# Matmuls of the identity issued at the matrix engine's long planned waits, in a four-layer transformer block over four sequences

## The chip, the cores and the metric

The kernel runs on one core of one Trainium2 chip. Its time is the device time of one execution in microseconds (us), the median over several executions. A core has a matrix engine, TensorE (PE in the profile; PEld is its loading of weights), a vector engine (DVE), a scalar engine (ACT), GpSimd (POOL), and SyncE (SP), which here only issues transfers. TensorE writes into PSUM, eight banks of 128 partitions by 2 KB (512 float32 columns each).

## What is computed

Four sequences of 1024 tokens with 256 features pass, each by itself, through causal attention, a gated feed-forward block, sliding-window attention (64 keys) and the same feed-forward block again, each behind a layer norm and with a residual sum:

```python
x = x + attn_a(layernorm(x))    # x @ W1 + b1; causal softmax, 16 heads of 16; @ Wp + bp
x = x + ffn(layernorm(x))       # silu(x @ Wg.T) * (x @ Wu.T) @ Wd.T; hidden 768, int weights / 127
x = x + attn_b(layernorm(x))    # window of 64 keys, the first 63 given as initial keys and values
x = x + ffn(layernorm(x))       # the same feed-forward weights
```

## The kernel before

The kernel counts eight "layers", numbered 0 to 7: for each sequence a causal attention with its feed-forward block (even numbers) and a sliding one with its own (odd numbers). Every float32 product that needs the precision is made from two parts, hi and lo, rounded apart.

**Events.** The work of a layer is cut into events, each with one or more steps on different engines. Those that matter here, by their letters in the code: `L` turns four normalised token tiles with eight transposes (line 1285); `L0` and `L1` come before attention for the two halves of the tokens, `L2` and `L3` before the feed-forward block. `Q` and `P` make queries, keys and values (L1337 to L1339, L1353 to L1356). `A` computes scores once for the row maxima, which DVE reduces (L1424 or L1390; L1019); `T` turns the maxima (L1581). `B` computes the scores again, transposed and with the maximum subtracted, for ACT's exponential (L1446; L1215), `V` weighs the values (L1474). Both run over eight groups of heads and token halves, so that `B(3,0)` is the first piece of group 3. `O` projects (L1493 to L1496), `G0` to `G11` are gate and up for twelve pieces of the hidden layer, six for each token half, eight matmuls of 512 columns each (L1514, L1515), then a Silu on ACT (L1253), a product on DVE (L1096), the hi part on ACT (L1268) and the lo part on POOL (L921). `W(h,p)` is the product with the down weights, 24 matmuls of 256 columns (L1529, L1534), which waits for the lo part of all six pieces of its half. The second half of the feed-forward block of one layer is interleaved with the start of the next layer (small letters `g`, `w`).

**Order.** A planner, `Plan.order` (line 418 and on), writes the order of every engine's steps and the PSUM banks of each event at build time. It holds a cost for each step (`steps`) and what each needs (`needs`), keeps `free[engine]` and `done[event, step]`, and picks greedily. A planned wait of TensorE is the difference between the start that it works out for the next PE step and `free["PE"]`. The plan exists in four versions: layer 0, odd layers, even layers, and layer 7. `released(bank)` is the planned time at which the holder of a bank has been read for the last time.

**Run.** TensorE's program walks that order in `run`. Each event waits for its inputs and, in `banks_free`, for the semaphores that tell that the former holders of its banks have been read (`BEFORE`, from `holders_before`). The program from `G0` of layer 0 on stands twice, behind a branch on a value read at run time: the second parts of the feed-forward weights are used only where they are not all zero. A check of 36 matmuls (L1559) of these second parts with themselves, and a maximum over the result, decides it.

Of the kernel before, what the change touches and what calls it, by code (L numbers as in the profile page):

```python
# [21 lines left out]
P = 128  # L22
# [3 lines left out]
W = 64  # L26
# [15 lines left out]
BANKS = 8  # L42
SWITCH = 0.1
REACH = 96
PIECES = 8
SET_BY_POOL = 19
LANDED = {('stats', 0): 0.0, ('stats', 1): 4.5, ('qkv',): 2.5, ('bq',): 4.0, ('att_b',): 7.5, ('bias',): 8.5, ('wp', 0): 8.5,
# [35 lines left out]
class Plan:  # L83
# [11 lines left out]
    def __init__(self, a):  # L95
        self.causal = a % 2 == 0
        self.opening, self.final = a == 0, a == LAYERS - 1
        if self.causal:
            self.keys = [range(4 * (hf + 1)) for hf in range(2)]
        else:  # L100
            self.keys = [range(4 * hf, 4 * hf + 5) for hf in range(2)]
        if self.causal:
            self.a_units = [[u for i in range(4 * hf, 4 * hf + 4) for u in self.units(i, self.a_width(i))]
                            for hf in range(2)]
        else:
            self.a_units = [[(i, 0, HG, REACH) for i in (4 * hf, 4 * hf + 2)] for hf in range(2)]
        self.b_units = [[u for j in self.keys[hf] for u in self.units(j, self.b_width(hf, j))]
                        for hf in range(2)]
        self.b_upto = [{j: 1 + max(n for n, u in enumerate(units) if u[0] == j) for j in keys}
                       for units, keys in zip(self.b_units, self.keys)]  # L110
        self.a_base = running([len(self.a_units[sg // 4]) for sg in range(SUPERS)])
        self.b_base = running([len(self.b_units[sg // 4]) for sg in range(SUPERS)])
        self.v_base = running([len(self.keys[sg // 4]) for sg in range(SUPERS)])
        self.key_tiles = [(sg, j) for sg in range(SUPERS) for j in self.keys[sg // 4]]
        self.chunks = 2 if self.causal else 3
        self.slots = 2 if self.causal else 4
        self.lns = [0, 1, 2, 3]
        self.tail = range(12 if self.final else 6)
        self.us, self.program, self.banks = self.order(LIKES[2 if self.opening else 0 if self.causal else 1])

    def units(self, tile, width):

# [296 lines left out]
    def order(self, like):  # L419
# [2 lines left out]
        free = {"PE": 0.0, "ACT": 2.0, "DVE": 2.0, "POOL": 3.0, "SP": 0.0}  # L422
        banks = {}
        holder = [None] * BANKS
        at_start = [0.0, 0.0, 0.0, 0.0, 1.0, 1.0, 2.0, 2.0]
        done, program = {}, {engine: [] for engine in free}
        if self.opening:
# [35 lines left out]
        while left:  # L463
            best = None
            for m, (events, n_steps) in enumerate(streams):
                for step in range(n_steps):
                    if at[m][step] == len(events) or step and at[m][step] >= at[m][step - 1]:
                        continue
                    e = events[at[m][step]]
                    kind = e[0]  # L470
                    steps = self.steps(e)
                    if step >= len(steps):
                        best = (-1.0, m, step, e, None, 0.0)
                        continue
                    needs = self.needs(e, step)
                    if any(x not in done for x in needs):
                        continue
                    start = max([free[steps[step][0]], done[e, step - 1] if step else 0.0] + [done[x] for x in needs])
                    if kind == "Z" and e[1] == 0 and not self.causal:
                        start = max(start, 3.0)  # L480
                    if kind == "g" and not step:
                        start = max(start, 1.0)
                    if not step and self.banks_of(e):
                        slot, _ = choice(e, start)
                        if slot is None:
                            continue
                        start = max(start, slot)
                    key = start - like[self.group_of(e)]
                    if steps[step][0] == "PE" and self.in_quarters(e) != quarters:
                        key += like["turn"]  # L490
                    if not step:
                        if kind in "AB":
                            key = max(key, free[steps[1][0]] - steps[0][1] - like[f"ahead{e[1] // 4}"])
                            if kind == "A" and reached["A"] > reached["B"] + like[f"lead{e[1] // 4}"]:
                                key += 1.5
                        if kind == "P" or kind == "Q" and e[2]:
                            key += -like["late"] if (("A", 0, 3 if self.causal else 1), 0) in done else 3.0
                    if best is None or key < best[0]:
                        best = (key, m, step, e, steps, start)
            key, m, step, e, steps, start = best  # L500
            at[m][step] += 1
            left -= 1
            if steps is None:
                continue
            engine, us, after = steps[step]
            if engine == "PE" and self.in_quarters(e) != quarters:
                quarters = not quarters
                us += SWITCH
            free[engine] = start + us
            done[e, step] = start + us + after  # L510
            program[engine].append((e, step))
            if not step:
                if self.banks_of(e):
                    banks[e] = choice(e, start)[1]
                    for bank in banks[e]:
                        holder[bank] = e
                if e[0] in reached:
                    hf = e[1] // 4
                    units = (self.a_units if e[0] == "A" else self.b_units)[hf]
                    reached[e[0]] = e[1] + (e[2] + 1) / len(units)  # L520
        self.done = done
        return max(free["PE"], free["ACT"] - 2.0, free["DVE"] - 2.0, free["POOL"] - 3.0,
                   done.get((("W", 0, 1), 1), 0.0) - 2.3), program, banks


_PLANS = {a: Plan(a) for a in (0, 1, 2, LAYERS - 1)}
# [11 lines left out]
def holders_before():  # L538


    held, out = {}, {}
    for a, plan in enumerate(PLANS):
        for e, step in plan.program["PE"]:
            if e in plan.banks and (a, e) not in out:
                out[a, e] = list(dict.fromkeys(held[bank] for bank in plan.banks[e] if bank in held))
                for bank in plan.banks[e]:
                    held[bank] = (a, e)
    return out


def next_tables():
# [4 lines left out]
    return {x: TABLES[y[1][0]] for x, y in zip(ops, ops[1:]) if TABLES[x[1][0]] != TABLES[y[1][0]]}  # L556


BEFORE = holders_before()
NEXT_TABLE = next_tables()  # L560


def layers_kernel(nc, x, att_a, att_b, b_qk, b_v, wp_a, wp_b, b_p, w_gu, w_dn, k_init, v_init, out):
# [5 lines left out]
    with ExitStack() as ctx:  # L569
# [71 lines left out]
        ident_b = sb("ident_b", [P, P], BF16)  # L641
# [637 lines left out]
        def _(pe):  # L1279
# [8 lines left out]

            def banks_free(a, e):


                for b, (kind, *n) in BEFORE.get((a, e), ()):
                    plan = PLANS[b]
                    if kind == "Q":
                        pe.wait_ge(part_rest, chunk(b, *n) + 2)
                    elif kind == "P":
                        pe.wait_ge(v_done, VALUE_DONE_BASE[b] + VALUE_DONE[b % 2][n[0]])
                    elif kind == "A":
                        pe.wait_ge(a_max, A_BASE[b] + plan.a_base[n[0]] + n[1] + 1)
                    elif kind == "T":  # L1300
                        pe.wait_ge(peak_done, SUPERS * b + n[0] + 1)
                    elif kind == "B":
                        pe.wait_ge(exp_done, B_BASE[b] + plan.b_base[n[0]] + n[1] + 1)
                    elif kind == "U":
                        if n[0] == "bias":
                            pe.wait_ge(s_bias, 3)
                        else:
                            pe.wait_ge(s_wide, 5)
                    elif kind == "V":
                        pe.wait_ge(o_copied, SUPERS * b + n[0] + 1)  # L1310
                    elif kind == "O":
                        pe.wait_ge(out_res, 4 * b + 2 * n[0] + 2)
                    elif kind == "L":
                        pe.wait_ge(xlo_done, 4 * b + n[0] + 1)
                    elif kind in "Gg":
                        pe.wait_ge(hid_done, 12 * (b if kind == "G" else b - 1) + n[0] + 1)
                    elif kind in "Ww":
                        pe.wait_ge(down_res, 4 * (b if kind == "W" else b - 1) + 2 * n[0] + n[1] + 1)
# [247 lines left out]
            def run(part, wide_weights=False):  # L1566
                for a, e, step in part:
                    kind = e[0]
                    if kind == "U":
                        set_up(a, e, step)  # L1570
                    elif kind == "A":
# [293 lines left out]
```

## Time and profile before

| | |
|---|---|
| median of 3 executions | 1346.78 us |
| lowest, highest | 1344.25, 1348.1 us |
| the profiled execution, its own time | 1348.13 us |
| its span in the profile | 1346.4 us |
| mean granted TensorE clock in it | 0.963 |
| PE busy | 1209.5 us |
| DVE busy | 860.4 us |
| ACT busy | 777.2 us |
| POOL busy | 417.6 us |

The granted clock is given as a share of full speed: 1.00 stands for 2.4 GHz and 0.50 for 1.2 GHz. Busy time of PE contains matmuls at either.

### The profile page before, as it was taken

The numbers are of one execution on the slowest core, as the hardware profiler recorded it, in microseconds if no ns is written. First come the engines' busy times: TensorE is split into PE (matmuls) and PEld (weight loads), VectorE is DVE, ScalarE is ACT, GpSimd is POOL, SyncE is SP. The second block draws the span as 40 slices with busy tenths as digits, with TensorE's granted clock in tenths as the row PEclk, the third lists the DMA queues.
The fourth block names the chain that finished last, engine by engine and source line by source line (L and its number), as shares of the span: only waits on it lengthen the run. The fifth ranks groups of instructions, "written<-read, shape, count | busy, mean of one in ns | idle before, by whom it ended". The sixth has DMA issues, their size and how long they took to land.

```text
span 1346.4 us, 28734 instructions
## 1 busy us (share of the span) xinstructions
PE 1209.5 (90%) x11393; PEld 791.4 (59%) x11393; DVE 860.4 (64%) x1544; ACT 777.2 (58%) x1125; POOL 417.6 (31%) x406
## 2 busy tenths in 40 slices
PE   5889989997999998987999998999799999898877
PEld 5433458776853337865884333886687433487666
DVE  5888735556689845555659883555567987355562
ACT  4546764564554674656456576555555566755652
POOL 6612533123441223411353112431235212332132
PEclk9999989998999998998899998999899999899989
DMA  6610402634340121444343030153426203026330
GB/s 236 185 33 26 158 26 86 165 109 142 103 133 14 58 79 64 120 112 137 110 137 95 2 119 18 63 152 97 135 97 171 61 10 120 24 75 168 89 99 32
DMA packets 108965, 129.96 MB, mean 97 GB/s; under 512 B 29632, under 2 KB 89088, under 8 KB 107904
## 3 DMA queue, kind: packets, MB, share of 16 engines
q1 hardware_dynamic: 108832, 128.11, 31.5%
q8 instruction: 93, 1.52, 0.5%
q14 instruction: 40, 0.33, 0.1%
HBM read 46.21 MB, written 11.61 MB: 43 GB/s over the span
## 4 chain that ended last, share of the span: by engine, by line
PE 62%; ACT 11%; DVE 11%; SPq 6%; issue 5%; POOL 3%; DMA 3%; POOLq 0%; ACTq 0%; DVEq 0%
PE ring L1474 10%; PE ring L1446 8%; PE ring L1514 7%; PE ring L1515 7%; DVE peak L1019 7%; PE ring L1424 6%; ACT probs_causal L1215 6%; SPq L1717 5%; PE ring L1529 4%; PE ring L1534 3%; PE ring L1371 3%; PE ring L1285 2%; PE ring L1337 2%; ACT L1121 2%; PE ring L1338 2%
## 5 line engine op out<-in xcount | busy, mean ns | idle before, releaser
L1019 DVE TENSOR_REDUCE peak<-ring 128x1 f32<-128x768 f32 (+8 forms) x416 | 405.1, 1011 | 83.8 <-PE ring L1371 64.6
L1215 ACT ACTIVATE probs_causal<-ring 128x1024 f32<-128x1024 f32 (+1 forms) x320 | 289.7, 940 | 173.5 <-PE ring L1446 153.3
L1446 PE MATMUL ring<-q_st,k_st 98*128 98x512 bf16 (+6 forms) x1408 | 242.8, 284 | 17.2 <-DMA q_st<-peak_b 7.5
L1424 PE MATMUL ring<-k_st,q_st 96*128 96x512 bf16 (+3 forms) x768 | 180.0, 329 | 17.9 <-DVE peak L1019 7.5
L1446 PEld LDWEIGHTS ring<-q_st,k_st 98*128 98x128 bf16 (+1 forms) x1408 | 101.1, 98 | 149.7 <-DVE peak L1019 41.0
L915 POOL TENSOR_TENSOR onf<-onf,o_hi 128x512 fp32r<-128x512 f32 x64 | 82.8, 1294 | 321.3 <-ACT o_hi L1235 321.3
L1514 PE MATMUL ring<-xt_hi,w_gu_sb 128*128 128x512 f32 x384 | 163.9, 427 | 20.7 <-DVE xt_lo L953 17.3
L909 POOL TENSOR_SCALAR_AFFINE_SELECT probs_causal<-probs_causal 128x512 f32<-128x512 f32 x128 | 82.7, 648 | 306.2 <-ACT probs_causal L1215 305.9
L921 POOL TENSOR_TENSOR h_lo<-hid,h_hi 128x512 fp32r<-128x512 f32 x96 | 122.4, 1288 | 158.0 <-ACT h_hi L1268 156.9
L1474 PE MATMUL ring<-probs_causal,V 128*32 128x512 f32 (+3 forms) x1536 | 162.3, 497 | 5.5 <-POOL probs_causal L909 4.8
L1515 PE MATMUL ring<-xt_lo,w_gu_sb 128*128 128x512 f32 x384 | 161.3, 420 | 0.0
L1215 ACT ACTIVATE probs_sliding<-ring 128x768 f32<-128x768 f32 (+3 forms) x160 | 101.5, 685 | 55.4 <-PE ring L1371 27.3
L1529 PE MATMUL ring<-w_dn_sb,h_hi 128*128 128x256 f32 x384 | 107.6, 313 | 23.8 <-POOL h_lo L921 23.8
L1096 DVE SCALAR_TENSOR_TENSOR hid<-ring,gate 128x512 f32<-128x512 f32 x96 | 65.6, 689 | 94.4 <-POOL h_lo L921 59.6
L1424 PEld LDWEIGHTS ring<-k_st,q_st 96*128 96x128 bf16 x768 | 56.8, 98 | 104.8 <-ACT probs_causal L1215 40.4
L1534 PE MATMUL ring<-w_dn_sb,h_lo 128*128 128x256 f32 x384 | 104.8, 306 | 0.0
L1514 PEld LDWEIGHTS ring<-xt_hi,w_gu_sb 128*128 128x128 f32 x384 | 80.0, 208 | 40.5 <-DVE xt_lo L953 19.2
L1253 ACT ACTIVATE gate<-ring 128x512 f32<-128x512 f32 x96 | 56.8, 596 | 75.8 <-PE ring L1515 75.4
L1529 PEld LDWEIGHTS ring<-w_dn_sb,h_hi 128*128 128x128 f32 x384 | 83.0, 216 | 28.3 <-issue 28.3
L1515 PEld LDWEIGHTS ring<-xt_lo,w_gu_sb 128*128 128x128 f32 x384 | 79.7, 207 | 17.0
L1371 PE MATMUL ring<-mask_a,ident_b 128*128 128x128 bf16 (+1 forms) x448 | 86.8, 228 | 0.0
L1534 PEld LDWEIGHTS ring<-w_dn_sb,h_lo 128*128 128x128 f32 x384 | 83.1, 216 | 0.0
(128 smaller groups left out, 1984.9 us busy)
## 6 DMA issues: line engine op xcount, KB each, us to landing
q_st<-q_part SPq DMA_DIRECT2D x192, 128.0 KB, 2.4
w_gu_sb<-img_gu SPq DMA_DIRECT2D x56, 384.0 KB, 4.8
k_st<-k_part SPq DMA_DIRECT2D x96, 144.0 KB, 2.5
k_st<-k_part SPq DMA_DIRECT2D x96, 128.0 KB, 2.4
w_qkv<-img_qkv SPq DMA_DIRECT2D x7, 1536.0 KB, 6.3
on_hi<-o_hi SPq DMA_DIRECT2D x64, 128.0 KB, 2.7
on_lo<-onf SPq DMA_DIRECT2D x64, 128.0 KB, 2.8
y<-X SPq DMA_DIRECT2D x8, 512.0 KB, 3.2
```

Source lines behind the costliest of these rows:

```text
L915: pool.tensor_tensor(o.bitcast(F32R), o, o_hi[:, sg % 2, :].bitcast(F32), ALU.subtract).then_inc(on_lo_done, 1)
L921: pool.tensor_tensor(h_lo[b % 2][m][:], hid[buffers][:, e[1] % 2, :], h_hi[b % 2][m][:].bitcast(F32), ALU.subtract).then_inc(h_lo_done, 1)
L1019: dve.tensor_reduce(dst, scores, AX.X, ALU.max).then_inc(a_max, 1)
L1215: act.activation(block[0:rows, n % slots, h:h + heads, 0:w], heads_of(flat_of(a, e), unit, w)[0:rows], ACT.Exp).then_inc(exp_done, 1)
L1371: last = pe.matmul(dst, ident_b[:, 0:rows], mask[:, None, :].to_broadcast([P, together, w]), start=False, stop=True, skip_group_check=True)
L1424: pe.matmul(psum[:, per * n + c:per * n + c + d], q, keys[0:SP_ROWS, head, W + c:W + c + d], start=(per * n % 512 == 0), stop=False, skip_ ...
L1446: last = pe.matmul(psum[0:rows, per * n:per * n + w], keys[:, head, first_key:first_key + rows], queries[:, head, q0 - HALF * hf:q1 - HALF ...
L1474: last = pe.matmul(ring[32 * h:32 * h + 32, bank, q0 - HALF * hf:q1 - HALF * hf], V[0:rows, j, HG * g + h, :, :].rearrange("p d o -> p (d ...
L1514: pe.matmul(dst, hi, xt_hi[:, kk, cols(h)], start=(kk == 0), stop=False)
L1515: last = pe.matmul(dst, hi, xt_lo[:, kk, cols(h)], start=False, stop=(kk == 1 and not wide_weights))
L1529: pe.matmul(dst, hi, w_dn_sb[:, m, 0:E], start=(m == 0 and t == 0), stop=False, skip_group_check=True)
L1534: last = pe.matmul(dst, lo, w_dn_sb[:, m, 0:E], start=False, stop=(m == M_HID - 1), skip_group_check=True)
```

## The change

Beside the order, the planner now notes every PE step ahead of which it foresees a wait of over 0.75 us, if some bank's last holder has been read by the planned start of that wait. It stores the bank that came free earliest and a count: the planned wait less 0.4 us, divided by 0.225 us, and at most 8. In TensorE's program, `keep_busy` is called ahead of each step except the set-up ones: it waits for the bank's last holder and then issues that many matmuls of the 128x128 bf16 identity, as the loaded weights, with the same identity four times over as 512 moving columns, into that bank. The result is not read. Order, banks, and everything on the other engines stay.

```diff
+LEAST, MARGIN, FILLER, MOST = 0.75, 0.4, 0.225, 8
 ...
             engine, us, after = steps[step]
+            if engine == "PE" and program["PE"]:
+                gap = start - free["PE"]
+                open_banks = [b for b in range(BANKS) if (released(b) or 1e9) <= free["PE"] and holder[b] is not None]
+                if gap > LEAST and open_banks:
+                    fill[e] = min(open_banks, key=released), min(int((gap - MARGIN) / FILLER), MOST)
 ...
         for e, step in plan.program["PE"]:
+            if e in plan.fill:
+                filled[a, e] = [held[plan.fill[e][0]]]
 ...
+            def keep_busy(a, e):
+                if (a, e) in FILLED:
+                    bank, count = PLANS[a].fill[e]
+                    wait_for(FILLED[a, e])
+                    for n in range(count):
+                        pe.matmul(ring[:, bank, :].rearrange("p (h c) -> p h c", h=4), ident_b[:],
+                                  ident_b[:, None, :].to_broadcast([P, 4, P]), start=True, stop=True,
+                                  skip_group_check=True)
 ...
             def run(part, wide_weights=False):
                 for a, e, step in part:
                     kind = e[0]
+                    if kind != "U":
+                        keep_busy(a, e)
```

(`wait_for` is the body that `banks_free` had.) Worked through the planner's own costs, the rule names these places, with the number of added matmuls ahead of each:

| layers | ahead of | sum of one layer |
|---|---|---|
| 0 | A(0,0) 2, A(1,1) 2, T(4) 3, B(4,0) 2, G0 8, W(0,0) 8 | 25 |
| 1, 3, 5 | L1 3, B(0,0) 3, V(5,7) 3, L2 8, G0 8, W(0,0) 3, L3 5 | 33 |
| 2, 4, 6 | B(3,0) 3, A(5,0) 1, V(7,6) 2, L2 8, G0 8, W(0,0) 3, L3 5 | 30 |
| 7 | as 1, 3 and 5, and W(1,0) 8 | 41 |

That is 56 places and 255 matmuls.

## Rows read from the trace of the kernel before

**Rows 1.** The page: busy time of each engine, and PE's granted clock in 40 slices

```profile
PE 1209.5 (90%) x11393; PEld 791.4 (59%) x11393; DVE 860.4 (64%) x1544; ACT 777.2 (58%) x1125; POOL 417.6 (31%) x406
PEclk9999989998999998998899998999899999899989
```

**Rows 2.** Windows: the 18 stretches at half clock; start:end, length, busy, PEclk, DMA

```profile
48.98:52.37 3.39, 3.39 (x17) 1.96 (x18) 2.01 (x4) 2.64 (x4) 1.42 (x2) 0.50 0.69 185
182.10:188.91 6.81, 5.99 (x14) 4.76 (x15) 2.11 (x4) 0.60 (x1) 0.33 (x1) 0.50 0.13 42
...
308.39:315.20 6.81, 5.07 (x12) 4.04 (x13) 5.04 (x8) 1.57 (x3) 1.27 (x1) 0.50 0.19 41
...
1335.81:1339.20 3.39, 3.39 (x18) 3.39 (x17) 0.00 (x0) 0.00 (x0) 0.00 (x0) 0.50 0.02 5
sum 98.63, PE 83.17 PEld 71.62 DVE 60.31 ACT 20.07 POOL 9.85; mean PE 4.62 PEld 3.98 DVE 3.35 ACT 1.11 POOL 0.55
```

**Rows 3.** Windows, sums alone: the seven stretches around G0, the seven behind W(0,0), layers 1 to 7

```profile
sum 57.88, PE 43.78 PEld 34.76 DVE 38.94 ACT 15.47 POOL 7.37; mean PE 6.25 PEld 4.97 DVE 5.56 ACT 2.21 POOL 1.05
...
sum 23.76, PE 23.23 PEld 23.35 DVE 15.45 ACT 1.16 POOL 0.73; mean PE 3.32 PEld 3.34 DVE 2.21 ACT 0.17 POOL 0.10
```

**Rows 4.** Timeline of PE, layer 1's feed-forward block: start, length, what, idle before and releaser

```profile
306.35 1.32 PE L1285 MATMUL ring<-ident,xn 128*128 128x128 f32 x8 [2.48 <-DVE xn L946]
310.13 0.77 PE L1514 MATMUL ring<-xt_hi,w_gu_sb 128*128 128x512 f32 x1 [2.46 <-DVE xt_lo L953]
...
316.24 0.40 PE L1514 MATMUL ring<-xt_hi,w_gu_sb 128*128 128x512 f32 x1
316.48 0.39 PE L1515 MATMUL ring<-xt_lo,w_gu_sb 128*128 128x512 f32 x1
...
329.06 0.55 PE L1529 MATMUL ring<-w_dn_sb,h_hi 128*128 128x256 f32 x1 [2.52 <-POOL h_lo L921]
...
333.42 1.04 PE L1285 MATMUL ring<-ident,xn 128*128 128x128 f32 x8
```

**Rows 5.** Waits of PE: for what, us in total, times, longest

```profile
PE ring L1529 <- POOL h_lo L921: 23.8, 9, 3.6
...
PE ring L1514 <- DVE xt_lo L953: 17.3, 7, 2.5
```

**Rows 6.** Timeline of PE, layer 3, and the granted clock around it by windows

```profile
584.72 0.40 PE L1446 MATMUL ring<-q_st,k_st 98*128 98x128 bf16 x4 [1.53 <-DMA q_st<-peak_b]
...
580.00:594.00 14.00, 10.70 (x325) 7.98 (x325) 5.31 (x11) 5.59 (x9) 0.00 (x0) 1.00 0.53 143
159.50:163.90 4.40, 4.40 (x44) 4.09 (x36) 2.82 (x10) 4.32 (x6) 3.11 (x3) 1.00 0.26 101
```

**Rows 7.** Timeline of PE: four 512-column bf16 matmuls at full clock, in layer 0

```profile
170.95 1.04 PE L1446 MATMUL ring<-q_st,k_st 98*128 98x512 bf16 x4
```

**Rows 8.** Timeline of PE: places of the change in layer 1 and in layer 2

```profile
236.65 0.99 PE L1285 MATMUL ring<-ident,xn 128*128 128x128 f32 x6
252.40 0.40 PE L1446 MATMUL ring<-q_st,k_st 98*128 98x128 bf16 x4 [0.24 <-DMA q_st<-peak_b]
...
408.14 0.60 PE L1446 MATMUL ring<-q_st,k_st 98*128 98x512 bf16 x2
...
504.43 1.32 PE L1285 MATMUL ring<-ident,xn 128*128 128x128 f32 x8 [1.14 <-DVE xn L946]
```

**Rows 9.** Timeline: G0 of layer 0 on PE, and the input that it needs, on DVE

```profile
182.92 0.76 PE L1514 MATMUL ring<-xt_hi,w_gu_sb 128*128 128x512 f32 x1 [3.43 <-issue]
...
180.59 1.23 DVE L953 TENSOR_TENSOR xt_lo<-ring,xt_hi 128x1024 fp32r<-128x1024 f32 x1 [9.85 <-ACT xt_hi L1115]
```

**Rows 10.** Timeline of ACT, POOL and DVE, what W(0,0) and L3 of layer 1 wait for

```profile
324.33 1.28 ACT L1121 ACT_TABLE_LOAD   x1
...
326.43 2.49 POOL L921 TENSOR_TENSOR h_lo<-hid,h_hi 128x512 fp32r<-128x512 f32 x2 [2.04 <-ACT h_hi L1268]
...
328.90 1.38 DVE L946 TENSOR_SCALAR xn<-X,mv,rstd 128x256 f32<-128x256 f32 x4
```

More of the change, by code:

```diff
@@ L118, in __init__ @@
         self.tail = range(12 if self.final else 6)
-        self.us, self.program, self.banks = self.order(LIKES[2 if self.opening else 0 if self.causal else 1])
+        self.us, self.program, self.banks, self.fill = self.order(LIKES[2 if self.opening else 0 if self.causal else 1])
     def units(self, tile, width):
@@ L424, in order @@
         holder = [None] * BANKS
+        fill = {}
         at_start = [0.0, 0.0, 0.0, 0.0, 1.0, 1.0, 2.0, 2.0]
@@ L522, in order @@
         return max(free["PE"], free["ACT"] - 2.0, free["DVE"] - 2.0, free["POOL"] - 3.0,
-                   done.get((("W", 0, 1), 1), 0.0) - 2.3), program, banks
+                   done.get((("W", 0, 1), 1), 0.0) - 2.3), program, banks, fill
 _PLANS = {a: Plan(a) for a in (0, 1, 2, LAYERS - 1)}
@@ L538, in holders_before @@
 def holders_before():
-    held, out = {}, {}
+    held, out, filled = {}, {}, {}
     for a, plan in enumerate(PLANS):
         for e, step in plan.program["PE"]:
+            if e in plan.fill:
+                filled[a, e] = [held[plan.fill[e][0]]]
             if e in plan.banks and (a, e) not in out:
@@ L547, in holders_before @@
                     held[bank] = (a, e)
-    return out
+    return out, filled
 def next_tables():
@@ L556, in next_tables @@
     return {x: TABLES[y[1][0]] for x, y in zip(ops, ops[1:]) if TABLES[x[1][0]] != TABLES[y[1][0]]}
-BEFORE = holders_before()
+BEFORE, FILLED = holders_before()
 NEXT_TABLE = next_tables()
@@ L1289, in banks_free, with wait_for @@
             def banks_free(a, e):
-                for b, (kind, *n) in BEFORE.get((a, e), ()):
+                wait_for(BEFORE.get((a, e), ()))
+            def keep_busy(a, e):
[6 more added lines that the diff above has]
+                                  skip_group_check=True)
+            def wait_for(holders):
+                for b, (kind, *n) in holders:
                     plan = PLANS[b]
```

## The prediction

> **What bounds the kernel now.** I read the page first, then TensorE's waits, then its clock, then the timeline where both meet. By the page PE is busy 90% of the span, with DVE at 64% next [rows 1]: TensorE carries the time, and what it saves or loses is mostly the kernel's. But part of its busy time runs at half clock. The windows find 18 stretches with a granted clock of 0.50 [rows 2]; 98.6 us together, in 83.2 of which PE works. As half of what runs at half clock would be left at full clock, these stretches hold 83.2 / 2 = 41.6 us. That is the most that the change can bring. (The opening, before 21.7 us, is slow too and has no added matmul.)
>
> Where do they lie? Sixteen of them at the feed-forward block, two in each layer: one around G0 and one behind the start of W(0,0); one early in layer 0, one at the very end. Layer 1 shows the pattern [rows 4]. PE waits 2.48 us for `xn`, turns it, waits 2.46 us for `xt_lo`, and G0 then begins at half clock: 12 matmuls take 5.07 us, 0.42 each [rows 2], against 0.24 or less at full clock [rows 4]. At 326.5 us it waits again, 2.52 us for POOL's lo parts, and W(0,0) starts at half clock. Both waits recur: 9 before L1529 with 23.8 us, 7 before L1514 with 17.3 [rows 5]. A shorter wait, 1.53 us in layer 3, lies in 14 us at full clock throughout [rows 6]. So what comes ahead of each fall at a feed-forward block is one wait of about 2.5 us or more.
>
> **The change, part by part.** It removes and moves nothing; DMA, ACT, DVE and POOL keep their work and order. It adds 255 matmuls at 56 places.
>
> *Price of one.* Four bf16 matmuls of 512 columns take 1.04 us with the tail of the last [rows 7], so about 0.22 us apart: 8 take 1.73 us, 5 take 1.08, 3 take 0.65. At half clock twice that.
>
> *Do they hold the clock?* No row shows the identity against itself. The nearest is the check L1559: for 4.4 us PE multiplies second parts which must be zero, since the third matmul of each `gate_up` never appears, and the clock stays 1.00 [rows 6]. So a matmul counts whatever its numbers are. With 8 of them, the waits ahead of L2 and G0 shrink from 2.48 and 2.46 us to some 0.75 each. Ahead of W(0,0) there are 3 only in layers 1 to 7: 2.52 - 0.65 = 1.87 us of idleness, between the 1.53 that did no harm and the 2.46 that did. I take it as harmless, being nearer to 1.53, and keep the other as a rival.
>
> *Gains.* Layers 1 to 7, around G0 and L2: 43.78 / 2 = 21.9 us [rows 3]. Behind it work waits for ACT and POOL: a table load and two lo parts stand between G5 and W(0,0) [rows 10]. POOL sat idle for 2.04 us before these two, so it can follow most of a 2.5 us shift; I take 19.5. W(0,0) of the same layers: 23.23 / 2 = 11.6 [rows 3]. W(0,0) of layer 0 and the last W(1,0), with 8 matmuls each: 1.7 + 1.7 (3.4 us of work in each stretch [rows 2]). The early stretch of layer 0, 3.39 us, has 2 matmuls some microseconds ahead of it: it may go or not, 0 to 1.7, I take 0.8. Sum 35.3.
>
> *G0 of layer 0* is another matter. Its 3.43 us are put down to "issue": `xt_lo` was done at 181.8 and G0 began only at 182.9 [rows 9], behind the branch. `keep_busy` comes behind the branch too, so the 8 matmuls begin when G0 could have begun, at a clock already at half since 182.1 [rows 2], and take 3.4 us. The stretch ends at the same time, so 3.4 us less of real work runs slowly in it: cost 3.4 - 1.7 = 1.7 us (between 0, if they fit before, and 3.4), and the 3.0 us of that stretch (5.99 / 2) are not gained.
>
> *Losses.* Where the plan foresees a wait that the chip does not have, the matmuls delay real work. L3: starts at 333.42 without a wait, behind W(0,0) [rows 4]. Its 5 matmuls cost up to 1.08 us in seven layers, 7.6. W(0,0) will end sooner, and its `xn`, ready at 330.3 us [rows 10], may then be what is late, so part of that time was waited anyway: I take 0.8 each, 5.6. L1 in four layers, no wait [rows 8]: 0.65 each, 2.6. B(0,0) in four, wait 0.24: 0.41 each, 1.6. L2 in layers 2, 4 and 6, wait 1.14 against 1.73: 0.59 each, 1.8. B(3,0) there, no wait: 0.65 each, 1.95; PE next waits for DVE's maxima, so I take 0.5 in all and keep 1.95 for the range. T(4) and B(4,0) in layer 0: 0.2. V(5,7), A(5,0), V(7,6), A(0,0): the wait covers them. Sum 12.3 (bounds 8 and 15.7).
>
> *Net.* 35.3 - 12.3 - 1.7 = 21.3 us. The profiled execution took 1348.1 us, so 1326.8 after; the median shown is 1.3 lower, so 1325.5. I say 1326 us.
>
> A page's rule would put the gain lower. The Trainium skill, TensorE: Matmul & The Clock Gate, Part 1, says that for modelling the cost of the slow start is under 1% of a typical span. By that at most 13.5 us could be had, and the sum would be about nil. The stretches of this kernel are 3.1% of its span by their own rows, and the sum goes by these.
>
> **The rivals.**
> (a) *W(0,0) still falls.* 1.87 us idle is enough for a fall. For it: the value lies between a harmless and a harmful one. Against: it is nearer to the harmless. The 11.6 us stay away; time 1346.8 - 9.7 = 1337. Chance 0.17.
> (b) *The feed-forward block goes at the pace of POOL and ACT*, so that a faster G0 only lengthens the wait before W(0,0). The 19.5 us vanish: 1346.8 - 1.8 = 1345. For it: W(0,0) always waits for POOL. Against: POOL is idle ahead of its last two parts [rows 10]. Chance 0.06.
> (c) *The added matmuls do not hold the clock* (the change doesn't do what it says), and this ends slower. All losses stay, 13.7 with a full L3, and G0's fill runs at half clock: 3.4 us in a wait of 2.46, 0.95 more in seven layers, half of it given back by the end of the slow stretch, 3.3; and 1.7 in layer 0: 1346.8 + 18.7 = 1365.5. It decides as soon as G0's first matmuls are still 0.42 apart. For it: no row shows a matmul of an identity by an identity; against it, the zero products [rows 6]. Chance 0.1.
> Layer 3's eight transposes belong to a stretch that stays at half clock. The Trainium skill, same page, Part 4, says that transposes do not count as busy in the usual way. The added ones are plain matmuls with an identity; if the chip took them for transposes, (c) would be the case, at 1365.5 us. In this trace the transposes alone never had to hold the clock, so it neither agrees nor disagrees.
>
> **How the numbers follow.** The forecast has 0.64, from 1316 (losses 8, all of G0's gain, the early stretch too: -30) to 1333 (losses 15.7, 3.4 in layer 0, 4 us of G0's gain lost: about -14). With (a) at 1337 the range goes to 1341: 1316 to 1341 leaves out (b), (c) and a rest of 0.03. About 0.3%, 4 us, can be told from no change: (b) is within it, (c) is slower. Faster 0.83, same 0.06, slower 0.11.
>
> **What would show it.** In the profile after: 255 more matmuls; granted clock near 0.99 with no 0.50 around G0 and W(0,0) of layers 1 to 7; G0's first matmuls 0.23 us apart; PE's waits before L1514 and L1529 cut from 17.3 and 23.8 us to under half; L3 starting behind its five matmuls. Layer 0's G0 should still be slow, with its eight added ones at 0.43 us. Windows at half clock behind W(0,0) would prove (a); waits before L1529 that grow by what G0 saves, (b); half clock in the added matmuls themselves all over, (c).

## The result, and the profile after

The changed kernel takes 1327.85 us (median of 4, 1325.64 to 1328.82) against 1345.51 for the kernel before on the same chip (median of 4, 1341.54 to 1348.1). The ratio is 0.9883, 95% interval 0.9862 to 0.9904 (it is not the quotient of the two medians, which would be 0.9869; by the ratio the gain is 15.7 us, by the medians 17.7). It was faster, by 16 to 18 us where 21 were forecast, and the median lies inside the range. In a second comparison further down the ratio was 0.9872 (0.9843 to 0.9900). The profiled execution took 1328.82 us, its span is 1327.1 us, 19.3 below that of before.

The page of the changed kernel, its lines for busy time and for the granted clock:

```profile
PE 1233.5 (93%) x11648; PEld 789.5 (59%) x11648; DVE 860.1 (65%) x1544; ACT 775.9 (58%) x1125; POOL 417.8 (31%) x406
PEclk9999999999999999999999999999999999999999
```

255 more matmuls, as the table says, and PE is *busier* by 24 us in a kernel that is 19 us shorter [rows 1]. DVE, ACT and POOL do the same work in the same time. The share of busy time would have told the wrong story here; the clock tells the right one. Each place where the granted clock goes from 1.00 to 0.50 is called a fall below. These are the stretches at half clock that are left, but for the one that only begins as the program ends (windows; length, busy times, granted clock):

```profile
69.96:73.35 3.39, 3.32 (x19) 0.88 (x19) 2.91 (x6) 0.50 (x1) 0.00 (x0) 0.50 0.50 160
182.60:185.99 3.39, 3.39 (x9) 1.92 (x8) 1.41 (x3) 0.00 (x0) 0.00 (x0) 0.50 0.26 83
325.96:329.35 3.39, 3.39 (x18) 3.39 (x18) 3.39 (x15) 0.00 (x0) 0.00 (x0) 0.50 0.67 278
844.78:848.18 3.40, 3.40 (x16) 2.88 (x16) 0.52 (x1) 0.00 (x0) 0.00 (x0) 0.50 0.40 170
971.08:974.47 3.39, 3.39 (x18) 3.39 (x17) 3.39 (x14) 0.00 (x0) 0.00 (x0) 0.50 0.79 332
1315.82:1319.21 3.39, 3.39 (x18) 3.39 (x17) 0.00 (x0) 0.00 (x0) 0.00 (x0) 0.50 0.02 5
sum 20.35, PE 20.28 PEld 15.85 DVE 11.62 ACT 0.50 POOL 0.00; mean PE 3.38 PEld 2.64 DVE 1.94 ACT 0.08 POOL 0.00
```

Eighteen stretches with 83.2 us of PE's work [rows 2] became six with 20.3, so by the forecast's own reckoning about (83.2 - 20.3) / 2 = 31 us were gained, and with 19.3 us less in the span some 12 of them were paid for elsewhere. Around G0 of layers 1 to 7 nothing is left. Behind the W's four stay: layers 1, 4, 5 and the last W(1,0). The timeline of PE in layer 1:

```profile
301.81 1.90 PE L1309 MATMUL ring<-ident_b 128*128 128x512 bf16 x8
304.34 1.32 PE L1294 MATMUL ring<-ident,xn 128*128 128x128 f32 x8 [0.64 <-DVE xn L955]
305.50 1.89 PE L1309 MATMUL ring<-ident_b 128*128 128x512 bf16 x8
308.12 0.47 PE L1538 MATMUL ring<-xt_hi,w_gu_sb 128*128 128x512 f32 x1 [0.74 <-DVE xt_lo L962]
308.43 0.40 PE L1539 MATMUL ring<-xt_lo,w_gu_sb 128*128 128x512 f32 x1
...
322.56 0.82 PE L1309 MATMUL ring<-ident_b 128*128 128x512 bf16 x3
325.25 0.35 PE L1553 MATMUL ring<-w_dn_sb,h_hi 128*128 128x256 f32 x1 [1.87 <-POOL h_lo L930]
...
329.69 1.25 PE L1309 MATMUL ring<-ident_b 128*128 128x512 bf16 x5
330.78 1.04 PE L1294 MATMUL ring<-ident,xn 128*128 128x128 f32 x8
```

Against [rows 4]: the waits of 2.48 and 2.46 us are 0.64 and 0.74, G0's matmuls come 0.24 us apart where they came 0.42 apart, and the delay from G0's start to W(0,0) went from 18.93 us to 17.13. Ahead of W(0,0) 1.87 us of waiting are left, and the clock falls at 326.0. Then come five matmuls ahead of L3, 1.09 us, for which nothing waited.

PE's waits (for what, us in total, times, longest) that answer to [rows 5]:

```profile
PE ring L1553 <- POOL h_lo L930: 15.7, 9, 1.9
...
PE ring L1538 <- DVE xt_lo L962: 5.2, 7, 0.7
```

The forecast named both as signs, to be cut to under half. The second was; the first was not, and could not be by the forecast's own waits: seven of 1.87 us, with some 0.8 and 1.9 us at the two places that have eight matmuls, are 15.8 us.

### The profile page after: what moved, and what is told of

Read it like the earlier page. It is cut to its first block, busy times and chain, and to the rows that moved or that the text cites. A ratio compares the mean times of both kernels' runs of the same rounds, so it can differ in the third digit from the quotient of the medians.

```text
span 1327.1 us, 29244 instructions
## 1 busy us (share of the span) xinstructions
PE 1233.5 (93%) x11648; PEld 789.5 (59%) x11648; DVE 860.1 (65%) x1544; ACT 775.9 (58%) x1125; POOL 417.8 (31%) x406
## 4 chain that ended last, share of the span: by engine, by line
PE 64%; ACT 10%; DVE 10%; issue 5%; SPq 5%; POOL 3%; DMA 2%; POOLq 0%; ACTq 0%; DVEq 0%
PE ring L1498 10%; PE ring L1470 9%; PE ring L1448 7%; PE ring L1538 6%; PE ring L1539 6%; DVE peak L1028 6%; ACT probs_causal L1224 6%; SPq L1743 4%; PE ring L1553 4%; PE ring L1558 3%; PE ring L1395 3%; PE ring L1361 2%; PE ring L1362 2%; PE ring L1363 2%; PE ring L1294 2%
## 5 line engine op out<-in xcount | busy, mean ns | idle before, releaser
L1538 PE MATMUL ring<-xt_hi,w_gu_sb 128*128 128x512 f32 x384 | 152.1, 396 | 5.9 <-DVE xt_lo L962 5.2
L1539 PE MATMUL ring<-xt_lo,w_gu_sb 128*128 128x512 f32 x384 | 150.1, 391 | 0.0
L1553 PE MATMUL ring<-w_dn_sb,h_hi 128*128 128x256 f32 x384 | 100.4, 298 | 15.7 <-POOL h_lo L930 15.7
L1558 PE MATMUL ring<-w_dn_sb,h_lo 128*128 128x256 f32 x384 | 98.3, 293 | 0.0
L1553 PEld LDWEIGHTS ring<-w_dn_sb,h_hi 128*128 128x128 f32 x384 | 77.3, 201 | 22.6 <-issue 22.6
L1538 PEld LDWEIGHTS ring<-xt_hi,w_gu_sb 128*128 128x128 f32 x384 | 72.4, 189 | 25.8 <-DVE xt_lo L962 8.4
L1539 PEld LDWEIGHTS ring<-xt_lo,w_gu_sb 128*128 128x128 f32 x384 | 72.4, 189 | 14.4
L962 DVE TENSOR_TENSOR xt_lo<-ring,xt_hi 128x1024 fp32r<-128x1024 f32 x32 | 39.2, 1224 | 63.6 <-ACT xt_hi L1124 63.6
```

Source lines behind the costliest of these rows:

```text
L1538: pe.matmul(dst, hi, xt_hi[:, kk, cols(h)], start=(kk == 0), stop=False)
L1539: last = pe.matmul(dst, hi, xt_lo[:, kk, cols(h)], start=False, stop=(kk == 1 and not wide_weights))
L1553: pe.matmul(dst, hi, w_dn_sb[:, m, 0:E], start=(m == 0 and t == 0), stop=False, skip_group_check=True)
L1558: last = pe.matmul(dst, lo, w_dn_sb[:, m, 0:E], start=False, stop=(m == M_HID - 1), skip_group_check=True)
```

## The experiments

Times are medians; a ratio, with its 95% interval, is to the kernel before, run beside it on the same chip. As above, it is not the quotient of the medians. The lines of code are those of the changed kernel's `keep_busy` unless said otherwise.

### 1. The same 255 matmuls with one column

```diff
-                        pe.matmul(ring[:, bank, :].rearrange("p (h c) -> p h c", h=4), ident_b[:],
-                                  ident_b[:, None, :].to_broadcast([P, 4, P]), start=True, stop=True,
+                        pe.matmul(ring[:, bank, 0:1], ident_b[:], ident_b[:, 0:1], start=True, stop=True,
```

> The 255 added matmuls stand at the same places but have 1 moving column in place of 512, so they keep TensorE at work for next to nothing. Theory (the gain comes from the clock, which matmuls of 512 columns hold up): the half-clock stretches around G0 and W(0,0) are all back, 16 to 18 of them with 98 us or so, G0's first matmuls 0.42 us apart, and the time is that of before, 1345 us, give or take 2. Rival (the gain comes from something else that the added code does, such as its waits on the bank's holder or the loading of the identity as weights, and the clock is a side effect): the time stays near 1328.

1341.26 us (10 runs) against 1341.51 (13 runs), ratio 0.9987 (0.9958 to 1.0016): nothing gained. Layer 1 on PE's timeline, and the sum over its 16 stretches at half clock by windows:

```profile
302.33 0.35 PE L1309 MATMUL ring<-ident_b 128*128 128x1 bf16 x8
304.88 1.31 PE L1294 MATMUL ring<-ident,xn 128*128 128x128 f32 x8 [2.19 <-DVE xn L955]
306.02 0.34 PE L1309 MATMUL ring<-ident_b 128*128 128x1 bf16 x8
308.65 0.77 PE L1537 MATMUL ring<-xt_hi,w_gu_sb 128*128 128x512 f32 x1 [2.29 <-DVE xt_lo L962]
309.22 0.63 PE L1538 MATMUL ring<-xt_lo,w_gu_sb 128*128 128x512 f32 x1
309.64 0.63 PE L1537 MATMUL ring<-xt_hi,w_gu_sb 128*128 128x512 f32 x1
...
sum 85.02, PE 72.91 PEld 63.65 DVE 48.49 ACT 10.31 POOL 6.82; mean PE 4.56 PEld 3.98 DVE 3.03 ACT 0.64 POOL 0.43
```

Same instructions, same waits on the banks' holders, same weight loads, but 0.35 us of work in place of 1.90: G0 is back at half clock. Fifteen of these stretches lie at the feed-forward blocks and one at the last W(1,0), 85 us together where the theory said 98; the early one of layer 0 is missing, and so is the one at W(0,0) of layer 7, behind a wait of 2.44 us. The gain of the change is the clock's, and it takes work of some length to get it.

### 2. Which of the places pay

Three kernels: without the matmuls ahead of L3; with those of the feed-forward block alone; with more of them at the W's. The two conditions and the count below are one of the three each.

```diff
-                if (a, e) in FILLED:
+                if (a, e) in FILLED and e != ("L", 3):
+                if (a, e) in FILLED and e in (("L", 2), ("G", 0), ("W", 0, 0), ("L", 3), ("W", 1, 0)):
                     bank, count = PLANS[a].fill[e]
+                    if e[0] == "W":
+                        count = 14 if e[1] else 10
```

> The change without its 5 matmuls ahead of L3 (seven layers, 35 matmuls fewer). In the changed kernel the step from W(0,0) to L3 shows about 1.1 us lost in each of them, with no wait before L3. Theory (pure loss, nothing to hold there): 7 x 1.1 = 7.7 us faster than the changed kernel, 1320 us, and no new half-clock stretch. Rival (DVE's norm becomes what is late, so the time was waited anyway): a wait of 0.5 us or more appears ahead of L3 and the gain is 3 us or less, 1325.

> The change with its added matmuls at the feed-forward block alone (L2, G0, W(0,0), L3, and W(1,0) of layer 7); those ahead of L1, B(0,0), V(5,7), B(3,0), A(5,0), V(7,6) and those in layer 0's attention are gone. In the changed kernel the delays at L1, B(0,0) and B(3,0) (0.6, 0.35 and 0.65 us) vanish again at the next wait of PE. Theory (they are absorbed): the same as the changed kernel within 2 us, 1326 to 1329, apart from the early stretch in layer 0, worth up to 1.7. Rival (they pass through, as the prediction had it, 2.6 + 1.6 + 0.5): 4 to 5 us faster, 1323.

> The change with 10 matmuls ahead of every W(0,0) in place of 3 (8 in layer 0) and 14 ahead of W(1,0) of layer 7 in place of 8. In the changed kernel the clock fell behind a remaining wait of 1.85 us at W(0,0) in layers 1, 4 and 5 and at W(1,0), and held at the same wait in layers 2, 3, 6 and 7. Theory (the remaining wait decides, and 1.85 us lies on the edge): no fall at any W, the waits left ahead of them 0.4 us or so, 3 x 1.5 + 1.7 = 6 us faster, 1322. Rival (the falls at W have another cause, such as the transfers in flight there): the same number of falls, and 1328.

Measured: 1321.87 (0.9833, 0.9778 to 0.9889), 1326.25 (0.9875, 0.9822 to 0.9928) and 1323.93 (0.9861, 0.9807 to 0.9915), against 1341.51 for the kernel before. The intervals are some 15 us wide and overlap each other and the change's, so the times alone separate none of these kernels from the change, and the traces decide.

*L3.* Without its five matmuls, the way from the start of W(0,0) to L3 in layer 2 on PE's timeline:

```profile
520.22 0.36 PE L1553 MATMUL ring<-w_dn_sb,h_hi 128*128 128x256 f32 x1 [1.85 <-POOL h_lo L930]
...
523.17 1.04 PE L1294 MATMUL ring<-ident,xn 128*128 128x128 f32 x8
```

2.95 us, with no wait ahead of L3. In the changed kernel the same way, also at full clock, takes 4.03:

```profile
521.70 0.35 PE L1553 MATMUL ring<-w_dn_sb,h_hi 128*128 128x256 f32 x1 [1.85 <-POOL h_lo L930]
...
524.64 1.25 PE L1309 MATMUL ring<-ident_b 128*128 128x512 bf16 x5
525.73 1.04 PE L1294 MATMUL ring<-ident,xn 128*128 128x128 f32 x8
```

So the five are a loss of 1.08 us in each of seven layers, 7.6 us, and `xn` is not late even then: PE waits ahead of L3 in no layer. Theory held.

*Attention.* The median of the feed-forward-only kernel, 1326.25 us, is what the first theory said and not the rival's 1323, but with this interval it refutes neither. What speaks for absorption is the changed kernel's trace, behind L1 of layer 1:

```profile
234.65 0.82 PE L1309 MATMUL ring<-ident_b 128*128 128x512 bf16 x3
235.30 1.04 PE L1294 MATMUL ring<-ident,xn 128*128 128x128 f32 x8
...
239.39 0.47 PE L1361 MATMUL ring<-xt_hi,w_qkv 128*128 128x512 f32 x1 [0.93 <-DVE xt_lo L962]
```

L1 is 0.60 us later by them than it was, relative to the work ahead; `Q(0,1)`, which waits 1.25 us before and 0.93 now, takes back 0.32, and the transposes, which no longer wait for one tile after another, 0.28. At B(3,0) the 0.65 us go into two waits for DVE's maxima, of 0.15 and 0.48 us, that shrink to nothing and 0.16. In layers 5 and 7 L1's 0.6 us are taken back at the same place.

*The W's.* With ten or fourteen matmuls no stretch at half clock is left from layer 1 to the end, and the wait ahead of W(0,0) is 0.35 us, ahead of W(1,0) 0.60. So it is the added work in the wait that keeps the clock up at W. The transfers are not the cause: they run there at 300 GB/s with the clock at full speed (windows, layer 1 of `more_at_w`):

```profile
325.00:332.00 7.00, 6.65 (x44) 4.65 (x44) 6.17 (x25) 0.61 (x2) 2.45 (x2) 1.00 0.80 300
```

The profiled execution still took 1323.78 us, 5 less than the change's: the two stretches of layer 0 are there as in the change.

### 3. Does it matter what is multiplied, and how

```diff
-                        pe.matmul(ring[:, bank, :].rearrange("p (h c) -> p h c", h=4), ident_b[:],
-                                  ident_b[:, None, :].to_broadcast([P, 4, P]), start=True, stop=True,
-                                  skip_group_check=True)
+                        pe.transpose(ring[:, bank, 0:P], ident[:], ident[:])
```

with `count` times 1.65, rounded. In the second kernel the matmul stays and both `ident_b` become `zeros_b`, a tile that POOL sets to zero at the start.

> Each added matmul is replaced by 1.65 transposes of the float32 identity (128 columns, 0.13 us each at full clock, the kind of L1285), so that TensorE is at work for as long as in the change, but with transposes. Theory A (any work of TensorE holds the clock): no half-clock stretch around G0, the time that of the change, 1328 us, within 3. Theory B (transposes don't count as work, as the Trainium skill says in TensorE: Matmul & The Clock Gate, Part 4): 16 or so stretches at half clock as before, the added transposes ahead of G0 running at 0.24 us each and past its wait of 2.46 us; with the losses at L3 (1.1 us in seven layers) the time is 1350 to 1360.

> The change with a tile of zeros in place of the identity, as weights and as moving data. Theory (what TensorE multiplies does not matter, as the zero products of the check in layer 0 suggested): as the change, 1328 us within 3, no fall around G0 of layers 1 to 7. Rival (the clock follows what the array really does with the data): falls around G0 as before, and 1350 us.

Transposes: 1324.06 us, 0.9862 (0.9835 to 0.9889). Zeros: 1328.62 us, 0.9891 (0.9866 to 0.9916). Both intervals contain the change's ratio. With transposes, layer 2 on PE's timeline and then by windows:

```profile
500.33 1.64 PE L1310 MATMUL ring<-ident 128*128 128x128 f32 x13
501.80 1.04 PE L1294 MATMUL ring<-ident,xn 128*128 128x128 f32 x8
502.68 1.58 PE L1310 MATMUL ring<-ident 128*128 128x128 f32 x13
505.31 0.47 PE L1537 MATMUL ring<-xt_hi,w_gu_sb 128*128 128x512 f32 x1 [1.05 <-DVE xt_lo L962]
505.62 0.40 PE L1538 MATMUL ring<-xt_lo,w_gu_sb 128*128 128x512 f32 x1
...
502.00:520.00 18.00, 16.82 (x98) 14.46 (x96) 10.61 (x22) 11.09 (x20) 8.48 (x7) 1.00 0.09 31
```

From 500.3 to 504.3 PE does nothing but 34 transposes, and G0 still starts at full clock; so it does in all of layers 1 to 7. The Trainium skill, TensorE: Matmul & The Clock Gate, Part 4, has it that transposes do not count as work in the usual way. For float32 transposes, and for keeping a clock that is at 1.00 already, this run shows the contrary, and the measurement decides. Whether transposes alone would bring the clock up from 0.50 no run here shows.

The same run holds a surprise at the W's. Five transposes are a little shorter than three matmuls and leave 1.97 us ahead of W(0,0), more than the change does, and yet the clock stays at 1.00 in all of layers 1 to 7. Only at W(1,0), with 2.22 us left, does it fall. Layer 2, PE's timeline and windows:

```profile
521.83 0.36 PE L1552 MATMUL ring<-w_dn_sb,h_hi 128*128 128x256 f32 x1 [1.97 <-POOL h_lo L930]
...
518.00:524.00 6.00, 4.03 (x34) 3.82 (x34) 4.87 (x15) 1.82 (x5) 2.94 (x3) 1.00 0.59 211
```

With zeros no stretch around G0 of layers 1 to 7 is at half clock either. Beside those at W and the one of layer 0 it has one ahead of L2 in layer 1, where `O` waits 2.31 us for a transfer and nothing is added.

### 4. Matmuls only where TensorE really waits

```diff
+COUNTS = {("L", 2): 8, ("G", 0): 10, ("W", 0, 0): 10, ("W", 1, 0): 14}
-                if (a, e) in FILLED:
-                    bank, count = PLANS[a].fill[e]
+                if (a, e) in FILLED and e in COUNTS:
+                    bank, count = PLANS[a].fill[e][0], COUNTS[e]
+                    if e == ("L", 2) and a % 2 == 0:
+                        count = 5
```

> Added matmuls only where TensorE waits long on the chip: 8 ahead of L2 (5 in even layers), 10 ahead of G0 and W(0,0), 14 ahead of W(1,0) of layer 7; none ahead of L3, L1, T(4) and the pieces of A, B and V. If the parts add up: 7.7 us less for L3, 4.5 to 6 for the falls at W that stay away, 0.8 for L2 in layers 2, 4 and 6, nothing for L1, B(0,0) and B(3,0): about 14 us faster than the change, a ratio to the kernel before of 0.977, and no half-clock stretch from layer 1 to the end. Rival (what one part saves another wait takes): 7 us faster than the change at most, 0.983.

> The trimmed kernel a second time, so that it stands beside the others on one chip: a ratio of 0.980 to the kernel before, within 0.002.

> The change itself a second time, beside the others on one chip: a ratio of 0.988 to the kernel before, within 0.002, and falls behind some of its eight waits of 1.85 us at W, not always the same ones, since the count was 4 of 8, 4 of 8 and 3 of 8 in three kernels with these waits.

1315.66 us, 0.9802 (0.9779 to 0.9824); the second time, beside the kernels of experiments 5 and 6, 1315.40, 0.9787 (0.9758 to 0.9816), where the change itself had 1326.77, 0.9872 (0.9843 to 0.9900). So 11.4 us less than the change on one chip, where the theory said 14 and the rival at most 7. The parts add up but for the falls at W: the theory counted three or four of them as saved, while the second profile of the change had only one. Between these two profiles the span goes from 1322.5 to 1313.2 us, 9.3 less, and 7.6 for L3, 1.7 for that one fall and 0.8 for L2 make 10.1. In `trimmed_again` PE's waits ahead of G0 and W(0,0) no longer stand among the seven largest, and one stretch at half clock is left before the end, in layer 0. (The first profile of the same kernel had one more, behind a wait of 2.12 us for a transfer ahead of O0 in layer 5; the theory had said none from layer 1 on.)

How often the clock falls behind the 1.85 to 1.90 us that the change leaves at its eight W's could be counted in five profiles: 4, 3, 4, 3 and 1 of 8 (the change, no L3, feed-forward only, zeros, the change again), 15 of 40. It is on the edge, and it is not always the same layers. Nor is the length of this wait all: the 1.97 us that the transposes leave brought no fall in seven cases.

### 5. Without the matmuls ahead of L2

```diff
-COUNTS = {("L", 2): 8, ("G", 0): 10, ("W", 0, 0): 10, ("W", 1, 0): 14}
+COUNTS = {("G", 0): 10, ("W", 0, 0): 10, ("W", 1, 0): 14}
```

> The trimmed one without its matmuls ahead of L2, so that the wait there is 2.48 us again in odd layers and 1.14 in even ones, followed by the transposes and the 10 matmuls ahead of G0. Theory (one wait of about 2.5 us can bring the clock down, 1.14 us can't): falls around L2 in layers 3, 5 and 7 and perhaps 1, none in layers 2, 4 and 6; where it falls, the 10 matmuls ahead of G0 run at half clock, 4.3 us in a wait of 2.5, so each fall costs 2 to 3 us: 6 to 10 us slower than the trimmed one. Rival (the matmuls ahead of G0 are enough): as the trimmed one within 2 us.

1319.27 us, 0.9804 (0.9766 to 0.9843): 3.9 us more than the trimmed one beside it, less than the theory's 6 to 10, with the intervals overlapping, so that the times do not tell the two kernels apart. Its trace has four falls around L2, in layers 1, 2, 3 and 4 and none in 5, 6 and 7, though PE waits there as in the others. Layer 2, and the same place in layer 7:

```profile
500.71 1.01 PE L1501 MATMUL ring<-probs_causal,V 128*32 128x256 f32 x16 [1.04 <-POOL probs_causal L919]
502.85 1.77 PE L1295 MATMUL ring<-ident,xn 128*128 128x128 f32 x8 [1.13 <-DVE xn L956]
504.42 3.35 PE L1312 MATMUL ring<-ident_b 128*128 128x512 bf16 x10
507.42 0.58 PE L1541 MATMUL ring<-xt_hi,w_gu_sb 128*128 128x512 f32 x1
...
1265.49 1.32 PE L1295 MATMUL ring<-ident,xn 128*128 128x128 f32 x8 [2.47 <-DVE xn L956]
```

The theory had said that 1.14 us can't bring the clock down. Two waits of 1.04 and 1.13 us with 1.0 us of work between them did in layers 2 and 4, not in layer 6, and the ten matmuls ran partly at half clock and past the wait. And the waits of 2.47 us, the length that the forecast blamed, did nothing in layers 5 and 7. So it is not the length of one wait alone that counts. The kernel before says so too. There the stretch of layer 2 begins 0.6 us into the wait for `xt_lo`, which runs from 505.75 to 508.21 us (PE's timeline, then windows):

```profile
508.21 0.77 PE L1514 MATMUL ring<-xt_hi,w_gu_sb 128*128 128x512 f32 x1 [2.46 <-DVE xt_lo L953]
...
506.37:513.17 6.80, 4.96 (x12) 3.92 (x13) 4.67 (x9) 1.56 (x3) 0.00 (x0) 0.50 0.03 5
```

Ahead of that wait lie only two of 1.05 and 1.14 us, with work between.

### 6. Layer 0

```diff
             pe.wait_ge(s_wide, 5)
+            fillers(ring[:, PLANS[0].fill["G", 0][0], :], 14)
             has_second = pe.value_load(wide[0:1, 0:1], min_val=0, max_val=1)
...
                     elif kind == "Q":
                         banks_free(a, e)
+                        if (a, e) == (0, ("Q", 0, 0)):
+                            fillers(ring[:, bank_of(a, e), :], 9)
```

`fillers` issues so many of the same matmuls; the ten of G0 of layer 0 behind the branch are gone. The second kernel has 8 ahead of the branch, and the 9 of the first Q go to bank 7, ahead of `banks_free`.

> As the trimmed one, and two places in layer 0: 9 matmuls ahead of the very first Q, whose wait is 4 us and whose 24 matmuls ran at half clock until 21.7 us in the kernel before; and for G0 of layer 0, 14 matmuls ahead of the branch in place of 10 behind it. Theory: the first Q runs at full clock from its start, worth 2 to 2.9 us if nothing else is late there, and G0 of layer 0 starts 1 to 2.6 us sooner and at full clock, worth 3 to 5 us against the matmuls behind the branch: together 5 to 7 us less than the trimmed one. Rival (the matmuls ahead of the branch hold up the reading of the value, since the read stands behind them): G0 starts 3 us later instead, and nothing is won there.

> As trimmed_and_start, mended at both places. The 9 matmuls ahead of the first Q go to bank 7, which nobody holds then, so that they start right behind the first transposes at 12 us and not behind xt_lo at 15.7; and 8 matmuls in place of 14 stand ahead of the branch, 1.7 us of work in a wait of 3.4. Theory (the 14 were too long, and the read of the value overlaps with them but for 1.6 us): G0 of layer 0 starts about 3.4 us behind the end of the transposes, as in the kernel before, and at full clock; the first Q starts at 15.8 and runs at 0.23 us a matmul: against the trimmed one 2 to 2.9 us there and 2.5 to 3 us at G0, together 5 us, a ratio of 0.976. Rival (the branch only begins to be fetched when TensorE is idle): G0 starts 1.7 + 3.4 us behind the transposes and nothing is won there, 0.978.

The first: 1314.48 us, 0.9793 (0.9769 to 0.9817), no gain that can be told. PE's timeline shows both faults:

```profile
15.73 4.02 PE L1305 MATMUL ring<-ident_b 128*128 128x512 bf16 x9 [3.94 <-DVE xt_lo L963]
19.19 0.99 PE L1367 MATMUL ring<-xt_hi,w_qkv 128*128 128x512 f32 x1
...
179.62 3.18 PE L1305 MATMUL ring<-ident_b 128*128 128x512 bf16 x14
184.36 0.47 PE L1544 MATMUL ring<-xt_hi,w_gu_sb 128*128 128x512 f32 x1 [1.55 <-issue]
```

The bank was still L0's, which holds it until `xt_lo` is read, so the nine matmuls came *after* the wait that they should fill, and the transposes behind the first 24 matmuls came 2.6 us later than in the trimmed kernel's profile. At the branch the fourteen did what the theory said: G0 came 1.55 us behind them, but 5.7 us behind the start of L2 where the trimmed kernel takes 8.1, and at full clock. The one fault took what the other place gave. The second, mended:

```profile
11.58 3.14 PE L1305 MATMUL ring<-ident_b 128*128 128x512 bf16 x9
15.82 0.47 PE L1367 MATMUL ring<-xt_hi,w_qkv 128*128 128x512 f32 x1 [1.10 <-DVE xt_lo L963]
16.12 0.40 PE L1368 MATMUL ring<-xt_lo,w_qkv 128*128 128x512 f32 x1
...
175.66 1.89 PE L1305 MATMUL ring<-ident_b 128*128 128x512 bf16 x8
179.63 0.47 PE L1544 MATMUL ring<-xt_hi,w_gu_sb 128*128 128x512 f32 x1 [2.09 <-issue]
```

1308.17 us, 0.9729 (0.9700 to 0.9757), 7.2 us less than the trimmed kernel beside it and 18.6 less than the change. The first Q starts at 15.82 as before, but at full clock: the next Q, twelve matmuls on, begins 2.45 us sooner. G0 of layer 0 comes 4.90 us behind the start of L2 (4.51 in the kernel before, 178.41 to 182.92), so that the eight matmuls are nearly hidden by the branch (neither 3.4 us behind the transposes' end nor 5.1, but 3.8: the reading overlaps with them in part). It starts at full clock, but 1.3 us later the clock falls once more, behind the 2.09 us that were left. This is the fastest of all the kernels. Its profile explains 4.1 us of the 7.2: W(0,0) of layer 0 starts at 197.79 us where the trimmed one's second profile has 201.89, near the 5 us of the theory. The rest is not located. The profiled execution, 1313.74 us, was the slowest of the six, and by its end only 1.2 us of the 4.1 were left, lost in waits of the attention parts where the kernels do not differ.

## Why the prediction was right, point by point

**The mechanism** was: the long waits in each feed-forward block bring PE's clock to half, and matmuls in them prevent it. Experiment 1 shows it: the same instructions with next to no work gain nothing. That numbers do not matter was argued from the zero products of the check; experiment 3 shows it. What the forecast had too simple is that one wait of about 2.5 us stands ahead of each fall: experiment 5 has the cases against it, and layer 2 of the kernel before, where the fall came 0.6 us into such a wait, was one from the start.

**The sum**, step by step, in the two profiled executions (a minus is a gain, in us; the shifts are those of the first matmul of each event against the kernel before; the row of the matmuls ahead of L2 is what the first matmul of L2 shifts against the last step ahead of it):

| step | predicted | measured |
|---|---|---|
| layer 0 up to G0 (early stretch) | -0.8 + 0.2 | -0.7 |
| G0 of layer 0 | +1.7 | +0.3 |
| the added matmuls ahead of L2, layers 2, 4 and 6 | +1.8 | +1.6 |
| L2 to W(0,0), layers 1 to 7 | -19.5 | -18.7 |
| W(0,0) to L3, layers 1 to 7 | -11.6 + 5.6 | +1.9 |
| W(0,0) of layer 0 | -1.7 | -1.5 |
| last W(1,0) | -1.7 | 0 |
| L1, B(0,0), B(3,0) and the rest of attention | +4.7 | -2.2 |
| sum | -21.3 | -19.3 |

**G0's term was right**, 18.7 where 19.5 was said. In layer 1, G2 starts 4.36 us sooner than before and W(0,0) only 3.81. Some 0.6 us is given back so in layers 1, 5 and 7 and nothing in the others, 1.7 in all, where the forecast took off 2.4. It put this down to POOL and ACT; what does it is not shown.

**The step that failed is the one at the W's**: "I take it as harmless, being nearer to 1.53". 1.85 us is not harmless but on the edge: the clock fell behind four of the eight, and in experiment 2, with a shorter wait, behind none. Rival (a) was half true. The same step took L3's five matmuls at 0.8 us, with DVE's norm late in their place; they cost 1.08 in full (experiment 2), 7.6 us in all. Together this is 9.6 us less than forecast, with the last W.

**Two errors went the other way, and the near hit of the sum owes much to them.** The 4.7 us at L1, B(0,0) and B(3,0) were said to pass through; where it was followed, the next waits absorbed them. The row's other 2.2 us of gain come from no term: the same stretches, from L3 of one layer to the last step ahead of L2 of the next, add up to anything from 4.8 us sooner to 1.5 later in the other profiles, one-column kernel and all, as PE's waits for transfers there vary. So 6.9 us of the sum are in part luck. And G0 of layer 0 cost 0.3 and not 1.7, because the clock came back after 3.4 us, where in the kernel before it had stayed down for 6.8 [rows 2]. That the added matmuls were work that brought it back is the likely reading, not a shown one: of ten profiles with full added work behind that branch eight have 3.4 us and two (zeros and the first of the trimmed kernel) 6.8, and the kernel before and the one-column kernel have 6.8 too. What the early stretch of layer 0 does is left open: at 49 us it was gone in the profile of the change, which had one at 70 instead; without any matmuls there, both profiles of the trimmed kernel had neither and the one of experiment 5 had it again. (And 1.4 us of gain came before the first added matmul, by a clock that rose at 18.8 us and not at 21.7; this is luck too, as other profiles of the same start have it anywhere between.)

**The rival that ended slower**, (c), is refuted by G0's matmuls, 0.24 us apart; its price had a slip, as the losses with a full L3 add up to 14.3 and not 13.7, which makes 1366 of its 1365.5. (b), that POOL sets the pace, is refuted by W(0,0) itself, which starts sooner by nearly all that G0 won.

The Trainium skill, TensorE: Matmul & The Clock Gate, Part 1, puts the slow start at under 1% of a typical span. That sentence is on the start alone, and the forecast was right not to go by it: what this kernel loses lies in the falls after it, 3.1% of its span, and the change took 1.2% off the time, the last kernel, with the first Q, 2.7%.

## What to carry to other kernels

Where an engine is the bound and the profile shows its clock below full speed, look at what stands ahead of each fall before looking at its busy share: here each fall cost 1.5 us at a W and 2.7 us at a G0, beside the wait itself. Work that nobody reads pays if it fits into a wait that the chip really has, leaves little of it idle (1.85 to 1.90 us were too much here in 15 of 40 cases; 0.3 to 1.05 left ahead of L2, G0 and W in none), and writes to a bank that is free at the wait's start. Put from a plan's foreseen waits, 56 places, it brought 1.2%; put at 25 waits read from the trace, 2.7%. Added work ahead of a step without a wait was a full loss where nothing waited behind it (L3) and none where something did (L1).

## What was not expected of the hardware

- The length of one wait does not settle whether the clock falls. 1.53 us in layer 3 did not bring it down, 1.85 to 1.90 did in 15 of 40 cases, 1.97 (experiment 3) in none of seven, 2.44 (one column, layer 7) did not, nor did 2.47 and 2.48 in layers 7 and 5 of experiment 5; but 1.04 and 1.13 us with 1.0 us of work between did, in two layers of three.
- Float32 transposes of an identity, and products of zeros, hold the clock as other matmuls do: with either, no stretch around G0 of layers 1 to 7 is at 0.50.
- The scatter of the kernel before is in part the clock's: beside the kernels of experiments 5 and 6 its executions went from 1339.66 to 1349.74 us, with a mean granted clock of 0.969 and 0.962. The fastest kernel still went from 1304.67 to 1313.74 at 0.998 to 1.000, so something else varies as well; this wasn't looked into.
- Matmuls ahead of a read that a branch hangs on lie beside it only in part: of 1.9 us of them, G0 was put off by 0.4, of 3.2 us by 1.15.
